# Two products of unit 4 on VectorE, four early maxima with their transpose and row moved forward, and x1 on ScalarE, in an attention and expert block on one core

## What is computed

```python
q, k, v = x @ Wq.T + bq, x @ Wk.T + bk, x @ Wv.T + bv      # 16 heads of 64
q, k = rope(q), rope(k)                                     # q * cos + rotate_half(q) * sin
attn = softmax(q @ k.T / 8)
x = layernorm(x + (attn @ v) @ Wo.T + bo)
gates = softmax(x @ gate_w)                                 # 8 experts, the best two count
h = gelu(x @ w1[e] + b1[e])
out = layernorm(x + sum over the best two e of (h @ w2[e] + b2[e]) * (sum of their gates))
```

## Time and profile before

| | |
|---|---|
| median of 3 runs | 226.55 us |
| the profiled execution, its own time | 227.77 us |
| its span, first to last instruction | 226.0 us |
| mean granted TensorE clock | 0.973 |
| busy: TensorE, VectorE, ScalarE, GpSimd | 170.3, 181.8, 166.5, 145.8 us |

### The profile page before, as it was taken

One profiled execution on the slowest core, in us unless ns is written; L12 is line 12 of the kernel. 1 busy time (PEld: TensorE's weight loads), 2 busy tenths in 40 slices (PEclk: granted clock), 3 DMA queues, 4 the chain that ended last, 5 costly groups with the idle time before them and its releaser, 6 DMA issues.

```text
span 226.0 us, 5252 instructions
## 1 busy us (share of the span) xinstructions
PE 170.3 (75%) x1820; PEld 124.7 (55%) x1839; DVE 181.8 (80%) x523; ACT 166.5 (74%) x346; POOL 145.8 (65%) x123
## 2 busy tenths in 40 slices
PE   1779775198677886777588678667696898999992
PEld 0223355166555774556466556545484675777781
DVE  6989965578579989896988989598979889486583
ACT  3878698069568977995797799578666799748624
POOL 6070869997939798987979897879960006012514
PEclk9999999859889999999999999999999999999998
DMA  6133503130202531212122131212120000001012
GB/s 238 76 84 91 135 23 73 35 83 20 60 18 62 176 76 43 60 38 59 38 61 69 39 74 47 62 35 60 38 61 1 1 4 4 0 3 46 0 51 93
DMA packets 13002, 12.63 MB, mean 56 GB/s; under 512 B 3152, under 2 KB 11952, under 8 KB 12976
## 3 DMA queue, kind: packets, MB, share of 16 engines
q1 hardware_dynamic: 12512, 11.77, 19.6%
q10 hardware_dynamic: 464, 0.52, 0.8%
HBM read 2.73 MB, written 1.05 MB: 17 GB/s over the span
## 4 chain that ended last, share of the span: by engine, by line
POOL 29%; DVE 27%; PE 25%; DMA 6%; ACT 6%; issue 5%; ACTq 1%; another core or an unknown queue 0%; POOLq 0%; DVEq 0%
POOL by_cos L1038 13%; POOL by_sin L1038 13%; DVE row_max L1209 8%; DVE roped L1170 7%; DMA qk<-mT_sb 6%; PE ps_o L598 5%; PE ps_s L563 4%; PE ps_m L505 4%; PE ps_t L453 3%; DVE o_sb L1232 3%; ACT raw L826 2%; DVE oT_sb L1262 2%; PE ps_m L386 1%; ACT probs L861 1%; ACT hg L986 1%
## 5 line engine op out<-in xcount | busy, mean ns | idle before, releaser
L861 ACT ACTIVATE probs<-ps_t 128x512 bf16<-128x512 f32 x128 | 77.0, 617 | 35.4 <-PE ps_t L453 34.8
L1209 DVE TENSOR_REDUCE row_max<-ps_s 128x2 bf16<-128x512 f32 x120 | 80.2, 673 | 15.7 <-PE ps_s L401 13.8
L1038 POOL TENSOR_TENSOR by_cos<-raw,in_b 128x1024 bf16<-128x1024 bf16 x26 | 55.2, 2122 | 17.6 <-DVE roped L1170 16.9
L401 PE MATMUL ps_s<-qk 128*128 128x256 bf16 x218 | 42.9, 280 | 19.7 <-DVE row_max L1209 19.0
L826 ACT ACTIVATE raw<-ps_m,bqk 128x256 bf16<-128x256 f32 x128 | 53.4, 486 | 4.8 <-PE ps_m L386 4.7
L453 PE MATMUL ps_t<-qk 128*128 128x256 bf16 x256 | 50.7, 283 | 7.8 <-DMA qk<-mT_sb 7.6
L1038 POOL TENSOR_TENSOR by_sin<-raw,in_b 128x1024 bf16<-128x1024 bf16 x26 | 55.2, 2123 | 0.0
L474 PE MATMUL ps_o<-v_sb,probs 128*128 128x65 bf16 x512 | 36.5, 195 | 2.4 <-DVE o_sb L1232 0.9
L474 PEld LDWEIGHTS ps_o<-v_sb,probs 128*128 128x128 bf16 x512 | 31.9, 99 | 7.4 <-ACT probs L861 1.2
L386 PE MATMUL ps_m<-in_b 128*128 128x256 bf16 x128 | 27.4, 307 | 8.4 <-DMA in_b<-in_packed_b 4.3
L453 PEld LDWEIGHTS ps_t<-qk 128*128 128x128 bf16 x256 | 23.4, 100 | 14.3 <-DMA qk<-mT_sb 9.8
(11 more groups left out here) (135 smaller groups left out, 242.9 us busy)
## 6 DMA issues: line engine op xcount, KB each, us to landing
qk<-roped SPq DMA_DIRECT2D x124, 64.0 KB, 2.0
in_b<-in_packed_b SPq DMA_DIRECT2D x1, 768.0 KB, 5.9
out<-y_sb SPq DMA_DIRECT2D x3, 256.0 KB, 2.2
in_f<-in_packed_f SPq DMA_DIRECT2D x1, 586.0 KB, 4.6
in_b<-in_packed_b SPq DMA_DIRECT2D x1, 512.0 KB, 4.5
in_b<-in_packed_b ACTq DMA_DIRECT2D x1, 256.0 KB, 3.7
qk<-mT_sb SPq DMA_DIRECT2D x16, 4.0 KB, 1.7
bv_rep<-in_repeated_bv SPq DMA_DIRECT2D x1, 256.0 KB, 2.9
```

What stands on the lines that cost most here:

```text
L401: mm = nc.tensor.matmul(ps_s[h % 2][:, t * S:t * S + S], qk[:, u % 4, 0, h % 4, h // 4, t * P:t * P + P], qk[:, u % 4, 1, h % 4, h // 4, : ...
L861: nc.scalar.activation(probs[:, h % 4].rearrange("p c s -> p (c s)"), ps_t[h % 2][:], ACT.Exp, scale=DH ** -0.5).then_inc(exp_done, 1)
L1038: last = nc.gpsimd.tensor_tensor(by[:, g].rearrange("p a h s -> p (a h) s"), raw[:, u % 2, g].rearrange("p a h s -> p (a h) s"), table[:]. ...
L1209: nc.vector.tensor_reduce(row_max[:, u % 2, h % 4, h // 4, :], of_head[:].rearrange("p (t s) -> p t s", s=S), AX_X, ALU.max, negate=True). ...
```

## The change

- EARLY is 4: steps 0 to 3 take heads 4 to 7 of unit T + 1, steps 4 to 7 heads 0 to 3 of unit T + 2. Slot 0 takes the head more, slot 1 has its own list.
- TensorE: the transpose of the maxima stands at the head of step 4. The maxima of step 1 stand ahead of the scores of step 0, and the P.V products of heads 6 and 7 of the unit before stand around those scores. The P.V product of head 2 waits until VectorE has copied the maxima out, since both are in one PSUM bank.
- VectorE: the copy of the maxima stands in step 4. In slot 1 VectorE makes the last two products of unit 4, and the rotation of unit 4 stands behind them. It splits the bias out of PSUM by three instructions. It makes the negated mean of batches 0 to 5 and no longer their x1.
- ScalarE makes x1 of batches 0 to 5, behind the exp of step 5 in odd slots, and reads no bias. It issues none of the copies of unit 2; SyncE issues all eight.
- GpSimd: two products of unit 4 instead of four, one bias instruction instead of five, and a multiplication (`shift1`) behind the power op of batches 0 to 5.
- SyncE: from slot 3 on the row of maxima goes ahead of all eight copies; before, three copies went ahead of it.

```diff
-EARLY = 3
+EARLY = 4
...
             if T == UNITS - 2:
-                return [(T + 1, h) for h in ((3, 4), (5, 6), (7,), (), (), (), (), ())[i]]
+                return [(T + 1, h) for h in ((4, 5), (6, 7), (), (), (), (), (), ())[i]]
+            if T == 1 and i >= UH - EARLY:
+                return [(3, h) for h in ((), (0,), (1,), (2, 3))[i - (UH - EARLY)]]
...
+        def pieces(u):
+
+            return 2 if u == 4 else 4
...
-                ahead = 3 if s["rotate"] and T >= 1 else 0
+                ahead = 3 if T in (1, 2) else 0
...
-                if (u, h) == (UNITS - 2, 2):
-                    pe.wait_ge(mT_ready, UNITS)
-                if (u, h) == (0, 2):
-                    pe.wait_ge(mT_ready, 2)
+                if h == 2 and u + 1 < UNITS:
+                    pe.wait_ge(mT_ready, u + 2)
...
                 find_scores(0)
+                find_scores(1)
+                if T == UNITS:
+                    turn_weights(0)
+                if T >= 1:
+                    times_v(T - 1, 6, it)
                 if s["attend"]:
                     scores(T, 0, it)
+                if T >= 1:
+                    times_v(T - 1, 7, it)
                 if s["out"] and T != 15:
                     out_proj((T - 3) // 2, it)
...
+                if s["maxima"] and T != 14:
+                    turn_maxima(T + 1, it)
                 find_scores(4)
...
+            def make_x1(b):
+
+                act.wait_ge(shift1_ready, b + 1)
+                for t in range(QT):
+                    last = nc.scalar.activation(x1[:, QT * b + t, :], ps_m[0][:, t * HID:t * HID + HID], ACT.Identity,
+                                                scale=rs1[:, t:t + 1], bias=shift1[:, t:t + 1])
+                last.then_inc(ln_step, 1)
...
                     exp(T, 5, it)
+                if s["out"] and T != 15:
+                    make_x1((T - 3) // 2)
...
                 nc.gpsimd.tensor_tensor(rs1[:, tiles], ve1[:, tiles], mhalf[:, tiles], ALU.pow).then_inc(rs1_ready, 1)
+                if b < LAST - 1:
+                    pool.wait_ge(rs1_ready, b + 1)
+                    nc.gpsimd.tensor_tensor(shift1[:], minus_mean1[:], rs1[:, tiles], ALU.mult).then_inc(shift1_ready, 1)
...
-                    for piece in range(4):
+                    for piece in range(pieces(T + 4)):
                         products(T + 4, piece)
+                if T == 1:
+                    third_part()
...
+            def split_bias():
+
+                whole = ps_m[1][:, 0:HID]
+                dve.wait_ge(bias_ready, 1)
+                nc.vector.tensor_copy(bias_p[:], whole).then_inc(bias_step, 1)
+                dve.wait_ge(bias_step, 1)
+                nc.vector.tensor_tensor(bias_r[64:P], whole[64:P], bias_p[64:P], ALU.subtract).then_inc(bias_step, 1)
+                dve.wait_ge(bias_step, 2)
+                nc.vector.tensor_tensor(bias_p[64:P], whole[64:P], bias_p[64:P], ALU.subtract).then_inc(bias_step, 1)
...
-                if s["rotate"]:
+                if s["rotate"] and T != 1:
                     rope(T + 3, 2)
                     rope(T + 3, 3)
...
                 find_maxima(4)
+                if s["maxima"] and T != 14:
+                    read_mT(T + 1, it)
+                if T == 1:
+                    dve.wait_ge(rope_ready, 8)
+                    products(4, slice(1, 2), by_cos, cos_sb, own_ready)
+                    products(4, slice(1, 2), by_sin, sin_sb, own_ready)
                 if s["attend"]:
                     normalise(T, 0, it)
+                if T == 1:
+                    rope(4, 2)
+                    rope(4, 3)
...
+            row_maxima(2, 3, 0)
+            split_bias()
             run(dve, slot)
```

More of the change, by code:

```diff
@@ L106, in postln_block @@
         ones_row = sb("ones_row", [1, P], BF16)
-        bias = sb("bias", [P, HID], F32)
         bias_r = sb("bias_r", [P, HID], F32)
@@ L126, in postln_block @@
         rs1 = sb("rs1", [P, 2 * QT], F32)
+        minus_mean1 = sb("minus_mean1", [P, QT], F32)
+        shift1 = sb("shift1", [P, QT], F32)
         half_b = sb("half_b", [P, QT], BF16)
@@ L195, in postln_block @@
         bias_ready = sem("bias_ready")
-        bias_read = sem("bias_read")
+        own_ready = sem("own_ready")
         bias_step = sem("bias_step")
@@ L225, in postln_block @@
         rs1_ready = sem("rs1_ready")
+        shift1_ready = sem("shift1_ready")
         x1T_psum = sem("x1T_psum")
@@ L351, in _ @@
             regroup(1)
-            sp.wait_ge(rope_ready, 6)
-            for g in range(2):
-                for half in range(2):
-                    sp.dma_start(qk[32 * half:32 * half + 32, 2, :, g],
-                                 roped[32 * g:32 * g + 32, 0, half]).then_inc(qk_in[2], 16)
+            regroup(2)
             slot(0, 0)
@@ L496, in out_proj @@
                 if b == 0:
-                    pe.wait_ge(bias_step, 5)
+                    pe.wait_ge(bias_step, 4)
                 for t in range(QT):
@@ L510, in biases @@
                 pe.wait_ge(bv_ready, 16)
-                take(1, bias_read, 1)
+                take(1, bias_step, 3)
                 nc.tensor.matmul(ps_m[1][:, 0:HID], ones_row[:], bo_sb[:], start=True, stop=False)
@@ L631, in slot @@
                     project(T + 4, 0, 0 if s["out"] else 1, 1)
-                if T >= 1:
-                    times_v(T - 1, 7, it)
                 find_scores(2)
@@ L679, in slot @@
                     times_v(T, 3, it)
-                if s["maxima"] and T != 14:
-                    turn_maxima(T + 1, it)
                 find_scores(6)
@@ L723, in first_slot @@
                 direct_maxima(1, [4, 5])
-                biases()
                 scores(0, 4, 0)
@@ L742, in first_slot @@
                 direct_maxima(2, [2])
+                direct_maxima(2, [3])
+                biases()
             for i in range(4):
@@ L823, in read_proj @@
                     act.wait_ge(products_ready, u - 4)
+                if g == 0 and a == 0 and u == 6:
+                    act.wait_ge(own_ready, 2)
                 for half in range(2):
@@ L877, in normed @@
                 last.then_inc(y_out, 1)
-            def read_bias():
-                act.wait_ge(bias_ready, 1)
-                nc.scalar.copy(bias[:], ps_m[1][:, 0:HID]).then_inc(bias_read, 1)
             def slot(T, it):
@@ L960, in _ @@
             read_value(2, 1, 0)
-            act.wait_ge(rope_ready, 6)
-            for g in range(2, 4):
-                for half in range(2):
-                    act.dma_start(qk[32 * half:32 * half + 32, 2, :, g],
-                                  roped[32 * g:32 * g + 32, 0, half]).then_inc(qk_in[2], 16)
-            read_bias()
             read_proj(4, 0, 0, 0)
@@ L1040, in products @@
                                                table[:].unsqueeze(1).broadcast_to([P, 4, S]), ALU.mult)
-                if piece == 3:
+                if piece == pieces(u) - 1:
                     last.then_inc(products_ready, 1)
@@ L1072, in route, with third_part @@
                 last.then_inc(g_step[r], 1)
-            def split_bias():
-                pool.wait_ge(bias_read, 1)
-                nc.gpsimd.tensor_copy(bias_p[:], bias[:]).then_inc(bias_step, 1)
-                pool.wait_ge(bias_step, 1)
-                nc.gpsimd.tensor_tensor(bias_r[64:P], bias[64:P], bias_p[64:P], ALU.subtract).then_inc(bias_step, 1)
-                pool.wait_ge(bias_step, 2)
-                nc.gpsimd.tensor_copy(bias_p[64:P], bias_r[64:P]).then_inc(bias_step, 1)
+            def third_part():
+                pool.wait_ge(products_ready, 3)
                 pool.wait_ge(bias_step, 3)
-                nc.gpsimd.tensor_tensor(bias_r[96:P], bias_r[96:P], bias_p[96:P], ALU.subtract).then_inc(bias_step, 1)
+                nc.gpsimd.tensor_tensor(bias_p[96:P], bias_r[96:P], bias_p[96:P], ALU.subtract).then_inc(bias_step, 1)
                 pool.wait_ge(bias_step, 4)
-                nc.gpsimd.tensor_copy(bias_p[96:P], bias_r[96:P]).then_inc(bias_step, 1)
-                pool.wait_ge(bias_step, 5)
             def slot(T, it):
@@ L1119, in _ @@
             slot(0, 0)
-            split_bias()
             run(pool, slot)
@@ L1197, in rope @@
                         dve.wait_ge(products_ready, u - 2)
+                    if u == 4:
+                        dve.wait_ge(own_ready, 2)
                     if u >= 2:
@@ L1250, in ln_one @@
                     dve.wait_ge(ln_step, LN_STEPS * b + 2)
+                    if b < LAST - 1:
+                        nc.vector.tensor_scalar(minus_mean1[:], mv1[:, 0:QT, 0], -1.0, None, ALU.mult)
                     last = nc.vector.tensor_scalar(ve1[:, 0:len(tiles)], mv1[:, 0:len(tiles), 1], EPS, None, ALU.add)
@@ L1357, in slot @@
                     route(0, 9)
-                if s["out"] and T != 15:
-                    ln_one((T - 3) // 2, 4)
                 if s["attend"]:
@@ L1376, in slot @@
                     route(1, 5)
```

(2 more changed lines are left out.)

5 lines of the change are left out of this document (removed).

## The result

The changed kernel takes **237.81 us** (median of 4 runs, 237.51 to 238.73); the kernel before took 226.55 in the same comparison (226.28 to 226.60). The ratio is 1.0507, 95% interval 1.0476 to 1.0538. The forecast was 229.3, with a range to 232.5: slower was right, but the loss is 11.3 us, not 2.7.

The account below looks back on a forecast made before the run. No engine is full; a loop of GpSimd's products and VectorE's rotation bounds the kernel. Terms -2.2 -2.1 +6.6 +0.1 +0.3 = +2.7 us on the profiled 227.77 give 230.5, forecast 229.3 against the median 226.55; range 223.5 to 232.5.

Parts of the forecast that it names:

- The turn's wait: Step four: TensorE's transpose of the maxima waits for the row maximum behind VectorE's rotation; everything behind comes 1.68 us later.
- raw(1,1): ScalarE's last copy of a unit's projection out of PSUM: at 6.74 us behind the odd slot's rotation, before 4.55.
- The B's: Five pieces from an odd slot's rotation to the even slot's, 9.77 us each before: +1.33 each, +6.6 in all.
- Products could be done by 10.05: GpSimd in a B: its shift op is hidden, so its products could end 10.05 us behind the odd slot's rotation.
- rotation at 11.1: End of a B: VectorE's row maximum and normalisation, then the even slot's rotation at 11.1 us, against 9.77.
- GpSimd stays the bound: Rival: ScalarE and TensorE catch up, B's fall to 10.05: 224.0 us, or 219 with A's at 9.77; chance 0.23.
- my signs for being right: Signs in the profile, among them GpSimd idle over 2 us ahead of the odd power op or the even products.
- The clock: Rival: TensorE idles late in the odd slots and its granted clock falls; 233 us with all five; chance 0.15.
- the first A: First piece from an even slot's rotation to the odd slot's: from 12.88 to 10.77 us, -2.1.
- The start: Up to unit 5's rotation: GpSimd loses two products and four bias ops, rotation at 50.8 instead of 53.03, -2.2 us.
- The A's: Pieces from an even slot's rotation to the odd slot's: 10.77 us each; the four behind the first 43.02 to 43.08, +0.1.
- The tail: Behind the last rotation, 68.22 us before: slots 12 and 13 pay the turn again, +0.3, between -1 and +1.

Follow-up runs that it names:

- Experiments 1 and 3: The change with the unit's last early maximum ahead of VectorE's rotation: 227.52 us, ratio 1.0001; the change with TensorE's transpose back at the end of step five: 229.26, 1.0032.
- experiment 4: The change with 14 matmuls (results not used) ahead of the transpose's wait in slots 2 to 13: 236.64 us, ratio 1.0364 to the kernel before.
- kernel 10: The change with the last early maximum ahead of the rotation, then copy of the maxima, row maximum, x1 back on VectorE: 222.09 us, ratio 0.9777 to the kernel before.
- kernel 1: The change with the unit's last early maximum read by VectorE ahead of the rotation: 227.52 us, ratio 1.0001 to the kernel before.
- experiment 6: The change with SyncE again putting three copies of a unit ahead of the row of maxima: 237.84 us, ratio 1.0491 to the kernel before.

## Why the prediction was wrong in size

**The turn's wait: right, to 0.1.** The transpose at 1.93 (2.04), exp five at 4.23 (4.35), raw(1,1) at 6.60 (6.74). Experiments 1 and 3 take the wait away from two sides and leave 1.0001 and 1.0032 of 1.0507.

**The B's: the step that failed.** "Products could be done by 10.05" and "rotation at 11.1". I had walked raw(1,1) to 6.74 and used it for TensorE's value projection, but not for GpSimd, whose last two products read it. My own numbers gave 6.74 + 0.84 for the op + 4.24 for two products = 11.82; measured 11.79. The 10.05 came from GpSimd's busy time, as if its inputs were always there. In the kernel before they were, but only just: raw(1,1) ended 5.39 behind the rotation and was wanted at 5.53 (the product at 91.41). The dropped dependency is 0.69 in each of five B's, **3.5 us**. It also answers the rival "GpSimd stays the bound": GpSimd was in the way, not by its work but by its wait. One of my signs for being right failed with it: GpSimd idle over 2 us ahead of the power op or the even products. It idled 1.52 and 1.41 there, and 1.89 between its second and third product.

**The clock: the rival came true in part.** It had a chance of 0.15 and a price of 4 us over the odd slots. Falls came in two B's at 0.51 each, one A at 0.98 and the first A, which stands 1.40 over the next A: at most **3.4 us**, of which experiment 4 shows 2.0 to be the falls behind the wait. One fall (108.45 to 120.23, granted clock 0.86) cost nothing. The first A's share is less sure: at full clock it took 10.79 in kernel 10 and 11.17 in kernel 1, 0.51 and 0.82 over the next A's there. By that estimate only 0.6 to 0.9 of the 1.40 is the clock's, and the rest is the first A's own, which the forecast, with one length for all A's, put at nothing.

**The start: nearly right.** 51.31 instead of 50.8, so 1.7 us are saved instead of 2.2. Unit 4's rotation came at 41.58, not 41.0: VectorE's list ahead of it took 0.6 more than I had added up (the three bias ops 0.97 instead of 0.8 of it). From there on GpSimd's products set the pace as forecast. It is kept in kernel 10 (51.32). No run made this part of the change alone.

**The A's: right, by luck in part.** At full clock 10.55 (10.77), GpSimd waiting for the rotation; the one fall made up the difference.

**The tail: too small,** +1.2 for +0.3. Slots 12 and 13 pay the same wait; it goes with the wait in the kernels compared in experiment 6, and SyncE's copies, which I suspected later, are not its cause.

In sum: -1.1 (A's at 10.55) +3.5 (the dropped wait) +3.4 (falls and the first A) +0.5 (start) +0.9 (tail) is, to rounding, the 7.1 between 2.7 and 9.8.
